# Another order on the sync queue: fills of the row buffers ahead of the denominators, in an attention kernel on one core

## What is computed

```python
x = x + conv3x3_grouped(gn(x), L0_conv_W)            # 32 groups
qkv = gn(x) @ w_qkv + b_qkv                          # 16 heads of 8
for a in range(7):
    for b in range(7):                               # 7x7 keys around each position, clipped at the edges
        logits.append(einsum('bnhwd,bnhwd->bnhw', q, k[ih, iw]) + rpb[:, bh, bw])
attn = softmax(stack(logits))                        # q was scaled by 8 ** -0.5
out = sum(attn[..., i] * v[ih, iw] for i in range(49))
x = x + out @ w_proj + b_proj
```

## Time and profile before

| | us |
|---|---|
| median of 3 executions | 1422.72 (1418.62 to 1424.17) |
| profiled execution, device time | 1416.9 |
| its span, first to last instruction | 1415.1 |
| PE busy in the span | 1150.5 (81%) |
| DVE busy | 882.1 (62%) |
| ACT busy | 674.9 (48%) |
| POOL busy | 596.1 (42%) |
| mean granted clock of TensorE, share of full speed | 0.85 |

### The profile page before, as it was taken

The page is one execution under the profiler, slowest core; times in us unless marked ns, Lnnn a source line. Parts: engine busy times, 40 slices in busy tenths (PEclk is TensorE's granted clock), DMA queues, the critical chain, the costliest instruction groups (busy, mean ns, idle before and its releaser), DMA issues.

```text
span 1415.1 us, 38250 instructions
## 1 busy us (share of the span) xinstructions
PE 1150.5 (81%) x12441; PEld 787.8 (56%) x12441; DVE 882.1 (62%) x2129; ACT 674.9 (48%) x1867; POOL 596.1 (42%) x1278
## 2 busy tenths in 40 slices
PE   3799999455889787888878887887889788878882
PEld 3555555353666565555656564655566565656561
DVE  3422222696777577667767775776667576757671
ACT  2100000602665556565756655565656465656652
POOL 3000000500647365454636473655546464637461
PEclk7699999655899798879989998998878889988886
DMA  9200000241546375645555464757455455645472
GB/s 260 53 34 31 33 32 32 75 109 20 135 105 173 73 181 109 161 114 126 146 113 135 105 157 84 181 99 177 104 136 133 110 141 107 152 97 148 94 177 58
DMA packets 142499, 159.59 MB, mean 113 GB/s; under 512 B 29953, under 2 KB 119889, under 8 KB 142041
## 3 DMA queue, kind: packets, MB, share of 16 engines
q1 hardware_dynamic: 141432, 153.13, 45.6%
q0 software_dynamic: 864, 3.90, 0.8%
HBM read 86.09 MB, written 70.47 MB: 111 GB/s over the span
## 4 chain that ended last, share of the span: by engine, by line
PE 58%; DMA 25%; DVE 9%; issue 5%; SPq 1%; POOL 0%; ACT 0%; DVEq 0%; POOLq 0%; ACTq 0%
DMA area<-mcol 23%; PE PS L1082 14%; PE PS L1187 12%; PE PS L1150 10%; PE PS L1171 6%; PE PS L1094 4%; PE PS L1135 4%; PE PS L1164 4%; DVE bias L935 3%; PE PS L1197 3%; DMA area<-x 2%; DVE area L977 1%; DVE mcol L988 1%; PE PS L1210 1%; PE PS L1063 1%
## 5 line engine op out<-in xcount | busy, mean ns | idle before, releaser
L572 POOL TENSOR_TENSOR halves<-masked 128x96 f32<-128x96 f32 (+1 forms) x512 | 204.7, 400 | 477.7 <-DVE masked L1009 477.3
L1150 PE MATMUL PS<-area 97*128 97x48 bf16 (+1 forms) x4112 | 258.1, 211 | 133.4 <-DMA area<-mcol 115.2
L998 DVE TENSOR_TENSOR S<-PS,bias 128x384 f32<-128x384 f32 (+1 forms) x513 | 283.7, 553 | 114.8 <-PE PS L1150 106.7
L748 ACT ACTIVATE VT<-PS 128x128 f32<-128x128 f32 x449 | 126.6, 282 | 403.8 <-PE PS L1135 402.4
L1150 PEld LDWEIGHTS PS<-area 97*128 97x128 bf16 x4112 | 187.1, 105 | 227.5 <-issue 162.0
L1187 PE MATMUL PS<-S,VT 128*36 128x96 f32 (+1 forms) x4096 | 302.0, 275 | 0.0
L755 ACT ACTIVATE S<-S 128x384 f32<-128x384 f32 (+1 forms) x512 | 274.6, 539 | 45.1 <-DVE S L998 31.8
L1187 PEld LDWEIGHTS PS<-S,VT 128*36 128x36 f32 x4096 | 182.1, 121 | 143.4 <-issue 94.7
L1009 DVE TENSOR_TENSOR masked<-PS,cst 128x192 f32<-128x192 f32 (+1 forms) x512 | 181.2, 354 | 95.2 <-PE PS L1187 89.5
L988 DVE TENSOR_REDUCE mcol<-PS 128x6 bf16<-128x480 f32 (+2 forms) x297 | 181.4, 611 | 94.5 <-PE PS L1171 94.5
L1082 PE MATMUL PS<-area 128*128 128x392 f32 x576 | 192.2, 497 | 3.9 <-DVE area L877 3.9
(11 more groups left out here) (87 smaller groups left out, 1141.8 us busy)
## 6 DMA issues: line engine op xcount, KB each, us to landing
k_parts<-area SPq DMA_DIRECT2D x204, 168.0 KB, 4.2
area<-k_parts SPq DMA_DIRECT2D x33, 1008.0 KB, 8.2
q_parts<-area SPq DMA_DIRECT2D x204, 98.0 KB, 2.3
area<-q_parts SPq DMA_DIRECT2D x66, 294.0 KB, 5.6
xa<-x_mid SPq DMA_DIRECT2D x18, 392.0 KB, 6.6
late<-x_mid SPq DMA_DIRECT2D x17, 392.0 KB, 8.4
out<-area SPq DMA_DIRECT2D x17, 392.0 KB, 8.1
den<-sums SPq DMA_DIRECT2D x66, 98.0 KB
```

Source lines behind the costliest of these rows:

```text
L572: nc.gpsimd.tensor_tensor(h, m[:, :, 0:2, :], m[:, :, 2:4, :], ALU.add).then_inc(s["half"], 1)
L998: nc.vector.tensor_tensor(S[:, n % 4, 0:cols], PS[:, SCORE + n % 2, 0:cols], bias[:, at:at + cols], ALU.add).then_inc(s["biased"], 1)
L1150: last = mm(PS[:, SCORE + n % 2, cols * g:cols * (g + 1)], key_rows[a][0:PEAK_ROW + 1, g, key:key + 128], query_rows[a][0:PEAK_ROW + 1, g, ...
```

## The change

Only SP's program and the counting of the rows change; no transfer is added, removed or resized.

- `store_parts` is cut in two, `store_keys` and `store_queries`, so that third key parts can be stored as soon as POOL has made them (`third` at 6i + 4) and third query parts later (6i + 6).
- In an even chunk, the key fill and the query fills of the next, odd chunk are issued at its start, ahead of the sums. Before, the query fills stood behind packed<-sums and the key fill behind den<-sums. The key fill of an odd chunk's buffer now waits itself until the buffer is free (all scores of the chunk before), which the later place gave before.
- In an odd chunk, the third key stores go ahead of the sums, the third query stores behind packed<-sums, the key fill follows them and stands ahead of sums<-packed; the query fills stay where they were, between den<-sums and the maxima.
- `rows_in` becomes `rows_in0` and `rows_in1`, one for each buffer, with three transfers each, and `outer_in` counts the outer maxima. PE waits for two semaphores at a chunk's head.

```diff
-        ROWS_IN = 16 * 4
+        ROWS_IN = 16 * 3
...
+            def store_keys(j, i, third):
+                wait(sp, "third" if third else "second", 6 * i + 4 if third else 3 * i + 2, j)
+                parts = (k1[i % 2], k23[0], k23[1])
+                for slot, (_, part) in enumerate(PAIRS):
+                    if (part == 2) == third:
+                        for l in range(2):
+                            sp.dma_start(k_parts[i % 2, l, slot].rearrange("d g n -> (d g) n"),
+                                         parts[part][64 * l:64 * l + 64, :]).then_inc(s["k_stored"], 16)
+            def store_queries(j, i, third):
+                wait(sp, "third" if third else "second", 6 * i + 6 if third else 3 * i + 3, j)
...
             def fill_keys(j, c):
                 if c % 2 == 0:
                     wait(sp, "k_stored", 192 * (c // 2 + 1), j)
+                else:
+                    wait(sp, "scores", TILES * (c - 1), j)
...
                 for c in range(4):
                     i = c // 2
-                    collect_denominators(j, c)
                     if c % 2:
-                        store_parts(j, i + 1, True)
-                    else:
+                        store_keys(j, i + 1, True)
+                        collect_denominators(j, c)
+                        store_queries(j, i + 1, True)
+                        fill_keys(j, c + 1)
+                        spread_reciprocals(j, c)
                         fill_queries(j, c + 1)
-                    spread_reciprocals(j, c)
-                    fill_keys(j, c + 1)
-                    if c % 2:
-                        fill_queries(j, c + 1)
-                    move_maxima(j, c + 1, False)
-                    move_maxima(j, c + 1, True)
-                    if c % 2 == 0:
-                        load_next((2 * j + i + 2) % IMAGES)
-                        store_parts(j, i + 1, False)
-                    else:
+                        move_maxima(j, c + 1, False)
+                        move_maxima(j, c + 1, True)
                         store(j, i, (2 * j + i + IMAGES - 1) % IMAGES)
                         load_residual(2 * j + i)
+                    else:
+                        fill_keys(j, c + 1)
+                        fill_queries(j, c + 1)
+                        collect_denominators(j, c)
+                        spread_reciprocals(j, c)
+                        move_maxima(j, c + 1, False)
+                        move_maxima(j, c + 1, True)
+                        load_next((2 * j + i + 2) % IMAGES)
+                        store_keys(j, i + 1, False)
+                        store_queries(j, i + 1, False)
...
                 if n == 0:
-                    wait(pe, "rows_in", ROWS_IN * (c + 1), j)
+                    wait(pe, f"rows_in{a}", ROWS_IN * (c // 2 + 1), j)
+                    wait(pe, "outer_in", 16 * (c + 1), j)
```

38 lines of the change are left out of this document (14 added, 24 removed).

## The result

The changed kernel takes 1426.74 us (median, 1425.72 to 1433.1); the kernel before, beside it, 1420.58. The ratio is **1.0059, 95% interval 1.0034 to 1.0085**: slower by 0.6%, where the prediction said 2% faster. The profiled execution has a span of 1428.3, 13.2 more than before.

What follows compares the result with a forecast made beforehand. PE sets the time, waiting 115.2 us at L1150, the first score tile of a chunk, mostly for the maxima; -31.9 (even wait) - 5 (clock) + 8 (odd chunks) = -29, so 1422.7 becomes 1394 us, range 1360 to 1434.

Steps and rivals of the forecast that it cites:

- The even wait, -31.9: Even chunks: with both fills at the chunk's start, PE's wait for the maxima goes whole, 16 x 2.0 us.
- The clock, -5: Even chunks: TensorE's clock drop ends sooner, 0.3 us a chunk, -5 us; bounds nothing and 28 us.
- Do the early fills make something else late? ... Cost taken: 0: Even chunks: sums and packed, behind the early fills, land by 615, reciprocal due at 615.1; it just fits, cost 0.
- The third key stores ... what this can delay it is in the bounds: Odd chunks: two key stores ahead of the sums, like 1.24 us of query stores; any reciprocal delay covered by the bounds.
- the odd chunks at +0.5: Odd chunks: +0.5 us each for both strands, 16 x 0.5 = +8 us; bounds -34 and +32.
- L, the landing of sums<-packed, 9.4: Odd chunks: sums<-packed, just behind the key fill, lands in 9.4 us instead of 1.56; bounds 6.8 and 10.9.
- Query fills and maxima, 5.7: Odd chunks, between reciprocal and restart: query fills take 5.6 us to land, the maxima with them, 5.7 in the sum.
- The signs I gave: Even maxima wait gone, maxima in 3 us; odd chunks: sums<-packed in about 9, DVE wait den<-sums some 4 at L1021.
- The even gain reappears as PE waiting within the next ten microseconds: Sign that the forecast is wrong: the even chunks' gain returns as PE or DVE waiting within ten microseconds.
- rival E: Even wait goes but DVE takes its place, odd chunks cost as forecast: +8 us, 1431; chance 0.05.

Runs made afterwards that it cites:

- even chunks alone: The changed kernel with odd chunks put back to the old order and even chunks kept as changed: 1417.36 us, ratio 1.001 against the kernel before.
- the foreign copy at the head: Kernel before plus a 1.57 MB copy to a spare tensor, which nothing waits for, issued in chunk 0: 1451.93 us; same copy in chunk 2: 1426.72.
- the first and third rows of the last table: Denominators' transfers moved to ACT's queue, on the kernel with chunk 0's fills behind packed<-sums; those fills issued 5.8 or 9.45 us after restart: 1390.16 and 1365.95 us.
- odd chunks alone: The changed kernel with even chunks put back to the old order and odd chunks kept as changed: 1416.22 us, ratio 0.996 against the kernel before.

## Why the prediction was wrong, point by point

- **The even wait, -31.9**: right as a wait. It went whole, and the maxima landed in 3.2 us. The time gained was less: with the clock's part the forecast had 2.3 us a chunk, chunk 2 gained 1.54, in "even chunks alone" 1.8.
- **The clock, -5**: the direction is as reasoned, a gain in time of its own is not shown. In the stretch behind DVE's wait TensorE still runs at the lower level (0.50, 1.2 GHz) for a part of the time, but climbs sooner. Windows (from:to, length, busy us and count of each engine, granted clock, DMA share, GB/s) of after, answering to the earlier trace rows:

```profile
566.70:568.40 1.70, 1.70 (x10) 0.75 (x10) 1.37 (x4) 0.63 (x1) 1.60 (x4) 0.68 0.92 315
568.50:572.00 3.50, 3.50 (x36) 2.07 (x36) 1.93 (x6) 1.76 (x5) 2.32 (x5) 0.68 0.87 280
```

0.68 where it was 0.50: 36 instructions in 3.5 us instead of 30.
- **"Do the early fills make something else late? ... Cost taken: 0"**: this step failed. It asked only whether the reciprocals would be late. In chunk 2 they are not. But in chunk 0 the engines branch back some 5 us behind the restart and load code over the same DMA engines, and that is work which no dependence shows. Cost: 2.8 us on average of the eight chunks 0, of which seven stand behind a branch, **+22** (PE's issue waits at this line grew by 22.8). The row for it was in the profile, PE's 2.25 us of "issue" at 606.00; I did not ask what that wait was for. Three things show it: the fills behind packed<-sums (-25 with the whole change around it), the foreign copy at the head against the same copy in chunk 2 (+25), and the first and third rows of the last table. The Trainium skill, page "DMA: Bandwidth & Descriptors", section "Queues, rings and completion order", says that each DMA engine takes turns between the queues it has work for, packet by packet, which would let a few code packets pass a megabyte of data quickly. The runs do not bear that out as a reason for no cost: the first code packet starts some 2 us later, and the step grew by 2.8 us.
- **"The third key stores ... what this can delay it is in the bounds"**, and the odd chunks at +0.5: this failed too, at the head of the sum. I counted from the reciprocal to the restart and took the reciprocal to come as long after the chunk's start as now. It hangs on SP, whose train starts and ends on its own time, and PE's earlier restart moves nothing there. With the train's last store 1.2 us later against the restart, the third key stores, which I priced at nothing, and the fill no longer fit in: the reciprocal came at 16.3 us behind the restart instead of 14.9, and sums<-packed went out at 17.0 instead of 15.4. It takes both parts of the change: "odd chunks alone" gains 0.3 a chunk, "even chunks alone" loses 1.0 by another path. Cost: +1.1 a chunk in place of +0.5, **+18** in place of +8; and about half of the even chunks' -2.0 comes back in the odd ones.
- **L, the landing of sums<-packed, 9.4**: measured 6.5, below my lower bound of 6.8 though only just. I had taken "issued behind a key fill" from the maxima, and they were issued 1.4 us behind it in the earlier trace rows. Sums<-packed lands with the fill, which here takes 7.1 us from an issue 0.8 ahead.
- **Query fills and maxima, 5.7**: the 5.6 us was the median over two kinds, 4.3 to 5.6 us in even chunks, where no key fill is ahead, and 8.7 to 10.9 in odd ones, behind a key fill; it holds for neither. Measured 8.3 from the first query fill's issue to the restart (24.9 to 33.3), probably since the fills now meet the output's and the residual's transfers and the key fill's tail; no run takes these apart. The two errors cancel: from the reciprocal to the restart it is 17.0 us, forecast 17.6.
- **The signs I gave**: the even wait gone, the maxima in 3 us, a new DVE wait for the denominators (3.08 in the row above, "some 4") all came. "The even gain reappears as PE waiting within the next ten microseconds" came as well, at the branch: the place of rival E, with another cause. Its number, 1431, is near the 1427 measured, by luck: DVE did not take the gain in even chunks; chunk 2 shows that.

The sum, remade with the measured terms: chunk 0 +0.75, chunk 1 +1.17, chunk 2 -1.54, chunk 3 +1.02, eight times, +11.2; the result in the medians is +6.2, in the profiled executions +13.2 (the one before was fast for its kernel, 1416.9 against a median of 1420.58, the one after slow, 1430.16 against 1426.74). Against the forecast's -29 this sum is 40 higher: 22 and 10 from the two failed terms, 8 from an even gain that came out smaller.

What stays open: the code's packets start late rather than take long, so they most likely stand behind the fill's packets in the DMA engines and not at the memory; no run separates the two. That the fills stopped PE and ACT and the foreign copy DVE goes with which code packets came late, all of them or all but the first; which packet holds which engine's code is not in the trace. And the path of the 1.0 us that the odd chunks lose in "even chunks alone" is only in part known.

## What to carry to other kernels

Before a large transfer is moved earlier, look at what has no dependence on anything and still needs the DMA engines: at a loop's head the engines load their code, and a wait marked "issue" there can be such a transfer; the rows of the instruction queues in the DMA view say when it starts. An order of issues has a length of its own: count the issues of the queue (here 0.65 us each) between the event that starts a chunk and the one the chunk hangs on, for when they fill the time, an engine that gets faster waits longer, and a second issuing queue brings what no order of the first can. Where a kernel has two such limits, try the two remedies apart, since together they can bring the small transfer behind the large one again.

## What the runs showed of the hardware that I had not expected

- **Code loading meets data.** The tile step with the branch back takes 4.4 to 4.9 us in quiet, where the same step without a branch takes 1.8; with 1.6 MB of fills in flight 7.2 to 8.7, with a foreign copy of 1.57 MB 2.3 us more in the next step.
- **Issuing costs more than moving.** Four stores of 98 KB an image taken off SP gave 34 us issued by ACT (1401.48 to 1367.03) and 37 left out; by the odd chunks 1.6 and 2.3 us each. The Trainium skill, page "DMA: Bandwidth & Descriptors", section "Issuing engines are not separate DMA queues", says that issuing on several engines saves only the sequencer's time, "which is usually small relative to the DMA itself". The first half agrees with the runs; here the small part was the one that counted.
- **A small transfer waits for a fill ahead of it.** Alone sums<-packed lands in 1.5 us, 0.8 us behind a key fill on the same queue in 6.2 to 6.9. On ACT's queue, with the key fill 0.5 us ahead on SP's, it takes 1.5 to 7.0 us, 4.2 on average, and 6.3 to 7.7 with the key fill 2 us ahead and the first query fill within 0.3 us of it. The maxima took 9.6 to 11.7 us behind three fills in the kernel before.
- **A store's form decides its price**: two 64-partition stores of one part take 1.3 us of SP's time, one 128-partition store of the same bytes 3.4 to 5.9, with the 16 DMA engines at a share of 0.13.
